# Attention with a mixture of experts on one core: VectorE copies the last transposed bank before the first block's maximum, and takes the norm sums and the token low parts in front of the context's copy

## The chip, the cores and the metric

The kernel runs on one core of a Trainium2 chip. The metric is the device time of one execution in microseconds; three runs of the kernel before gave 652.37, 653.87 and 654.20 us, with a median of 653.87 us. Everything below about where time goes comes from one further execution, taken by the hardware profiler: it took 654.04 us, and its span from the first to the last instruction is 652.0 us.

## The reference

Sixteen batches of 256 tokens with 128 channels go through a pre-norm block: causal attention with 16 heads (key width 8, value width 64), then a mixture of 8 experts that each pick their own 64 tokens.

```python
x = x + attn(layernorm(x), Wq, Wk, Wv, Wo)
x = x + ffn(layernorm(x), gate_w, w1, w2)

# attn: B, T, D = 16, 256, 128; H, DK, DV = 16, 8, 64
q, k, v = heads(x @ Wq), heads(x @ Wk), heads(x @ Wv)
attn = softmax(where(causal, -inf, q @ k.T / sqrt(DK)))
return (attn @ v) @ Wo

# ffn: E = 8, capacity 64 tokens of a batch for each expert
probs = softmax(x @ gate_w)
top_p, top_idx = top_k(probs.T, 64)
y = gelu(x[top_idx] @ w1) @ w2 * top_p
out[top_idx] += y
```

## The kernel before, in words

`attention` does the first half and the norm and the gate product of the second; `experts` follows it. The change is in `attention` alone, and there in VectorE's program alone.

**Units.** The 16 heads are cut in 4 groups of 4 heads, so that there are 64 units (`u = 4 * b + j`, with `b` the batch and `j` from 0 to 3). Each engine has its own program, written out by hand: a loop over `b` from -2 to 18 (the middle ones by a hardware loop), and in it the four values of `j`. The engines meet at semaphores only. In the step `u` an engine works on several units at once, each at another stage: queries and keys of `u + 2` (and on TensorE the product for `u + 3`), scores and exponentials of `u + 1`, transposed probabilities of `u - 1`, the context of `u - 2`.

**One unit.** TensorE makes the product for queries and keys (L635), ScalarE takes its high part (`qk_hi`, L352), VectorE the two low parts `qT` and `kT` (L449, L452). GpSimd spreads the keys over the heads' rows (`k_diag`, L303 and L305). TensorE multiplies: `s0_ps` are the scores of the first 128 queries (L620, L621), `s1_ps` those of the second 128 (L555 to L563). VectorE takes each row's maximum (L457 for the second block, L498 for the first), ScalarE the exponentials and their sums (L340), VectorE the reciprocals (`inv`, L480 and L522), GpSimd the normed probabilities (`probn`, L295 for the first block and L320 for the second). TensorE transposes them in three banks: two with L579 and L580, the third with L614. ScalarE copies two of the banks into `probT` (L362, L380), VectorE the third (L519). TensorE makes the context (L597), and VectorE copies it into `ctxT` (L486).

**Once for each batch.** At `j == 2` VectorE takes the sums of the first norm for batch `b + 2` (`norm_stats`, L505 to L511), GpSimd makes their root (L309, L311), and at `j == 0` of the next batch VectorE norms the tokens (`xn1`, L490, by the helper's line L434) and TensorE transposes them (L644). After the output product (L542) and the first residual (L476) at `j == 3`, VectorE takes the sums of the second norm (L512 to L515), GpSimd makes their root at `j == 0` (L314, L316), VectorE norms at `j == 1` (`xn2`, L495, again L434), and TensorE transposes (L650). ScalarE writes the high part of these tokens at `j == 2` (`xg_hi`, L383) and VectorE the low part (`xg_lo`, L503).

**What orders VectorE's work around the change.** Its instructions run in the written order. In a step this is: `qT` and `kT`; the second block's maximum (L457); one small piece by `j`; the first reciprocal (L480); the context's copy (L486); the norm itself at `j == 0` and `j == 1`; the first block's maximum (L498); then the low part and the sums; the third bank's copy (L519); the second reciprocal (L522). GpSimd's order in a step is `probn` of the first block (L295), `k_diag` (L303, L305), the roots, `probn` of the second block (L320).

Of the kernel before, what the change touches and what calls it, by code (L numbers as in the profile page):

```python
# [9 lines left out]
ALU = mybir.AluOpType  # L10
# [4 lines left out]
B, T, D = 16, 256, 128  # L15
TB = T // P
# [5 lines left out]
UNITS = B * G  # L22
# [8 lines left out]
def has(index, n):  # L31

    return not isinstance(index, int) or 0 <= index < n

def await_count(engine, sem, count):

    if not isinstance(count, int) or count > 0:
        engine.wait_ge(sem, count)
# [10 lines left out]
def f32(ap):  # L50
    return ap.bitcast(F32)
# [29 lines left out]
def attention(nc, x_tiles, w_q, w_k, w_v, w_o, gate_w, w1, w2,  # L81
# [5 lines left out]
    with ExitStack() as ctx:  # L87
# [34 lines left out]
        bn6 = sb("bn6", [P, TB, 6])  # L122
        mv1 = sb("mv1", [P, TB, 2])
# [3 lines left out]
        bn6b = sb("bn6b", [P, TB, 6])  # L127
        mv2 = sb("mv2", [P, TB, 2])
# [260 lines left out]
        def _(dve):  # L389
# [31 lines left out]
            def norm_stats(src, bn, mv, bn_done, bn_count, stats_done):  # L421
                nc.vector.memset(holds_wait[:, :], 0.0)
                for tb in range(TB):
                    last = nc.vector.bn_stats(bn[:, tb, :], src(tb))
                last.then_inc(bn_done, 1)
                dve.wait_ge(bn_done, bn_count)
                nc.vector.memset(holds_wait[:, :], 0.0)
                for tb in range(TB):
                    last = nc.vector.bn_aggr(mv[:, tb, :], bn[:, tb, :])
                last.then_inc(stats_done, 1)  # L430

            def norm(dst, src, mv, rstd, done):
                for tb in range(TB):
                    last = nc.vector.tensor_scalar(dst[:, tb, :], src(tb), mv[:, tb, 0:1], rstd[:, tb:tb + 1],  # L434
                                                   ALU.subtract, ALU.mult)
                last.then_inc(done, 1)

            def batch(b, par):
                for j in range(G):
                    u = b * G + j  # L440
                    r1, r2, rm = (j + 1) % RING, j % RING, (j + 1) % RING
                    if has(u + 2, UNITS):
                        w = u + 2
                        qk_ps = misc_ps[(3 * j) % 2][:, :].rearrange("p (a t) -> p a t", a=2)
                        dve.wait_ge(qk_hi_done, w + 1)
                        await_count(dve, s1_done, w - 1)
                        await_count(dve, k_ready, w - 1)

                        nc.vector.scalar_tensor_tensor(out=qT[r2][:, :], in0=f32(qk_hi[r2][:, 0, :]),  # L449
                                                       scalar=minus_low[:, 0:1], in1=qk_ps[:, 0, :],  # L450
                                                       op0=ALU.mult, op1=ALU.add)
                        nc.vector.scalar_tensor_tensor(out=kT[r2][:, :], in0=f32(qk_hi[r2][:, 1, :]),  # L452
                                                       scalar=minus_low[:, 1:2], in1=qk_ps[:, 1, :],
                                                       op0=ALU.mult, op1=ALU.add).then_inc(qk_ready, 1)
                    if has(u + 1, UNITS):
                        dve.wait_ge(s1_done, u + 2)
                        nc.vector.tensor_reduce(out=neg_max[:, r1, 1, :], in_=s1_ps[:, :, :], axis=AX.X,  # L457
                                                op=ALU.max, negate=True).then_inc(max1, 1)

                    extra = misc_ps[(3 * j + 1) % 2]  # L460
                    if j == 0 and has(b - 3, B):
                        dve.wait_ge(gate_done, b - 2)
                        nc.vector.tensor_copy(gate_logit[:, bass.ds((b - 3) * TB, TB), :],
                                              extra[:, 0:TB * E].rearrange("p (t e) -> p t e", t=TB)).then_inc(gate_ready, 1)
                    if j == 1 and has(b + 1, B):
                        dve.wait_ge(xT_hi_done, b + 2)
                        nc.vector.tensor_tensor(xT_lo[1 - par][:, :], extra[:, 0:T], f32(xT_hi[1 - par][:, :]),  # L467
                                                ALU.subtract).then_inc(xT_ready, 1)
                    if j == 2 and has(b - 2, B):
                        dve.wait_ge(x2T_done, b - 1)  # L470
                        await_count(dve, gate_done, b - 2)
                        nc.vector.tensor_copy(xn2T[:, :], extra[:, 0:T]).then_inc(x2T_ready, 1)  # L472
                    if j == 3 and has(b - 1, B):
                        tiles = bass.ds((b - 1) * TB, TB)
                        dve.wait_ge(wo_done, b)
                        nc.vector.tensor_tensor(x_all[:, tiles, :], extra[:, 0:T].rearrange("p (t d) -> p t d", t=TB),  # L476
                                                x_all[:, tiles, :], ALU.add).then_inc(x1_ready, 1)
                    if has(u + 1, UNITS):
                        dve.wait_ge(exp0, u + 2)
                        nc.vector.reciprocal(inv[:, r1, 0, :], sums[:, r1, 0, :]).then_inc(inv0, 1)  # L480
                    if has(u - 2, UNITS):
                        cb = par if j >= 2 else 1 - par
                        g = (j - 2) % G
                        dve.wait_ge(ctx_done, u - 1)
                        await_count(dve, wo_done, b - 1 if j >= 2 else b - 2)
                        nc.vector.tensor_copy(ctxT[cb][:, 2 * g:2 * g + 2, :], ctx_ps[:, :, :]).then_inc(ctx_ready, 1)  # L486
                    if j == 0 and has(b + 1, B):
                        dve.wait_ge(rstd1_done, b + 2)
                        await_count(dve, xT_done, b + 1)
                        norm(xn1, lambda tb: x_all[:, (b + 1) * TB + tb, :], mv1, rstd1, xn1_ready)  # L490
                    if j == 1 and has(b - 2, B):
                        dve.wait_ge(rstd2_done, b - 1)
                        await_count(dve, x2T_done, b - 2)
                        await_count(dve, xg_lo_done, b - 2)
                        norm(xn2, lambda tb: x_all[:, (b - 2) * TB + tb, :], mv2, rstd2, xn2_ready)  # L495
                    if has(u + 2, UNITS):
                        dve.wait_ge(s0_done, u + 3)
                        nc.vector.tensor_reduce(out=neg_max[:, r2, 0, :], in_=s0_ps[:, :, :], axis=AX.X,  # L498
                                                op=ALU.max, negate=True).then_inc(max0, 1)
                    if j == 2 and has(b - 2, B):  # L500
                        dve.wait_ge(xg_hi_done, b - 1)
                        tiles = bass.ds((b - 2) * TB, TB)
                        nc.vector.tensor_tensor(xg_lo[:, tiles, :], xn2[:, :, :], f32(xg_hi[:, tiles, :]),  # L503
                                                ALU.subtract).then_inc(xg_lo_done, 1)
                    if j == 2 and has(b + 2, B):  # L505
                        if isinstance(b, int) and b == -2:
                            dve.wait_ge(x_loaded[0], 16)
                        if isinstance(b, int) and b == 2:
                            for i in range(1, 4):
                                dve.wait_ge(x_loaded[i], 16)  # L510
                        norm_stats(lambda tb: x_all[:, (b + 2) * TB + tb, :], bn6, mv1, bn1_done, b + 3, stats1)  # L511
                    if j == 3 and has(b - 1, B):  # L512
                        dve.wait_ge(x1_ready, b)
                        await_count(dve, rstd2_done, b - 1)
                        norm_stats(lambda tb: x_all[:, (b - 1) * TB + tb, :], bn6b, mv2, bn2_done, b, stats2)  # L515
                    if has(u - 1, UNITS):
                        dve.wait_ge(t_done, (u - 1) * 3 + 3)
                        await_count(dve, ctx_done, u - 2)
                        nc.vector.tensor_copy(probT[rm][:, 1024:1536], t_ps[rm][:, :]).then_inc(t_dve, 1)  # L519
                    if has(u + 1, UNITS):  # L520
                        dve.wait_ge(exp1, u + 2)
                        nc.vector.reciprocal(inv[:, r1, 1, :], sums[:, r1, 1, :]).then_inc(inv1, 1)  # L522
# [517 lines left out]
```

## Time and profile before

| | |
|---|---|
| median of three runs | 653.87 us (652.37 to 654.20) |
| profiled execution | 654.04 us, span 652.0 us |
| TensorE matmul busy | 587.1 us, 90% of the span |
| VectorE busy | 433.9 us, 67% |
| ScalarE busy | 418.0 us, 64% |
| GpSimd busy | 350.2 us, 54% |
| mean granted clock of TensorE | 0.974 of full speed |

The attention half runs to about 475 us, in a pattern that repeats every 27.5 us (one batch, four steps). The experts take the rest. A row of the timeline gives the start and the length of an instruction, its engine, its line, what it writes and reads, and how long its engine had idled before it and for whom; instructions overlap at their edges by some 0.08 us. A busy TensorE does not mean a TensorE without pauses: a pause shorter than the modelled end of the matmul before it does not show as idle time, only as a wider distance between two starts.

### The profile page before, as it was taken

How to read it: one execution, taken by the hardware profiler on the slowest of the kernel's cores; microseconds unless marked ns; L12 is line 12 of the kernel's file. 1: busy time of each engine (PE TensorE's matmuls, PEld its weight loads, DVE VectorE, ACT ScalarE, POOL GpSimd, SP SyncE). 2: the span in 40 equal slices, each digit the busy share in tenths (PEclk: the TensorE clock that was granted, in tenths of full speed). 3: DMA queues.
4: the chain of work that ended last, by engine and by line, in shares of the span. 5: the costliest groups of instructions: out<-in, count | busy, mean ns of one | idle time of the engine just before them, and what ended most of it. 6: DMA issues, size and time to landing. Idle time of an engine off the chain costs nothing. (4 is left out here: it accounts for less than half of the span.)

```text
span 652.0 us, 15348 instructions
## 1 busy us (share of the span) xinstructions
PE 587.1 (90%) x5252; PEld 481.3 (74%) x5252; DVE 433.9 (67%) x1073; ACT 418.0 (64%) x1418; POOL 350.2 (54%) x373
## 2 busy tenths in 40 slices
PE   1799999999999999999999999999615999999996
PEld 1577877778777787877878778787503898989896
DVE  3578687787877878788787877966476233434245
ACT  2599797787977878778787787877021643334330
POOL 4577677666776768667686686766160010111111
PEclk9999999999999999999999999999956999999998
DMA  9600000000000000000000000000002100100001
GB/s 269 190 2 1 2 3 2 1 2 2 2 2 0 0 0 0 0 0 0 0 0 0 0 0 0 2 1 1 2 0 65 34 19 13 30 17 10 17 18 50
DMA packets 13548, 12.28 MB, mean 19 GB/s; under 512 B 832, under 2 KB 10304, under 8 KB 13504
## 3 DMA queue, kind: packets, MB, share of 16 engines
q1 hardware_dynamic: 13504, 11.69, 6.1%
q8 instruction: 28, 0.46, 0.3%
q14 instruction: 16, 0.13, 0.1%
HBM read 9.57 MB, written 2.11 MB: 18 GB/s over the span
## 5 line engine op out<-in xcount | busy, mean ns | idle before, releaser
L340 ACT ACTIVATE prob<-s_ps,neg_max 128x128 f32<-128x128 f32 (+1 forms) x512 | 209.0, 430 | 28.5 <-DVE neg_max L457 20.5
L303 POOL TENSOR_TENSOR k_diag<-kT,own_block 128x512 fp32r<-128x512 f32 x64 | 66.5, 1040 | 116.2 <-DVE kT L452 115.0
L320 POOL TENSOR_TENSOR probn<-prob,inv 128x1024 f32<-128x1024 f32 x64 | 121.2, 1894 | 2.6 <-DVE inv L522 2.6
L340 ACT ACTIVATION_READ_ACCUMULATOR prob<-s_ps,neg_max 128x1 f32 x512 | 110.2, 215 | 0.0
L597 PE MATMUL ctx_ps<-probT,v_sb 128*64 128x256 f32 (+1 forms) x1024 | 97.3, 332 | 0.8 <-DVE probT L519 0.8
L798 POOL TENSOR_TENSOR y_parts<-y_sb,y_parts 128x512 fp32r<-128x512 f32 x16 | 20.6, 1286 | 137.9 <-ACT y_parts L814 137.9
L597 PEld LDWEIGHTS ctx_ps<-probT,v_sb 128*64 128x64 f32 x1024 | 63.5, 136 | 30.0 <-issue 11.6
L457 DVE TENSOR_REDUCE neg_max<-s_ps 128x4 f32<-128x1024 f32 x64 | 77.8, 1216 | 0.4 <-PE s_ps L563 0.3
L498 DVE TENSOR_REDUCE neg_max<-s_ps 128x4 f32<-128x512 f32 x64 | 44.0, 688 | 48.4 <-PE s_ps L621 48.4
L295 POOL TENSOR_TENSOR probn<-prob,inv 128x512 f32<-128x512 f32 x64 | 66.6, 1040 | 11.5 <-PE t_ps L614 11.5
L486 DVE COPY ctxT<-ctx_ps 128x512 f32<-128x512 f32 x64 | 44.2, 690 | 33.2 <-PE ctx_ps L597 32.0
L362 ACT ACTIVATE probT<-t_ps 128x512 f32<-128x512 f32 x64 | 39.0, 609 | 41.1 <-PE t_ps L580 41.1
L579 PE MATMUL t_ps<-ident,probn 128*128 128x128 f32 x256 | 63.8, 287 | 1.3 <-DVE probT L519 1.0
L542 PE MATMUL misc_ps<-wo_sb,ctxT 128*128 128x128 f32 x512 | 63.5, 278 | 0.6 <-DVE xn2T L472 0.6
L542 PEld LDWEIGHTS misc_ps<-wo_sb,ctxT 128*128 128x128 f32 x512 | 59.6, 191 | 2.2 <-issue 0.8
L580 PE MATMUL t_ps<-ident,probn 128*128 128x128 f32 x256 | 60.2, 273 | 0.0
L1005 PE MATMUL y_ps<-w_sb,w_raw 128*64 128x128 f32 x1024 | 59.4, 274 | 0.0
L1005 PEld LDWEIGHTS y_ps<-w_sb,w_raw 128*64 128x64 f32 x1024 | 55.6, 137 | 2.2
L822 ACT ACTIVATE xin_hi<-pick_hi_ps 128x512 fp32r<-128x512 f32 x16 | 9.6, 599 | 72.4 <-PE pick_lo_ps L969 72.4
L833 ACT ACTIVATE w_raw<-h_ps 128x512 f32<-128x512 f32 x64 | 38.2, 598 | 26.1 <-PE h_ps L990 23.7
L535 PE MATMUL misc_ps<-xT_hi,wqk_hi 128*128 128x256 f32 x128 | 49.7, 388 | 1.0 <-DVE xT_lo L467 1.0
L352 ACT ACTIVATE qk_hi<-misc_ps 128x512 fp32r<-128x512 f32 x64 | 39.1, 611 | 15.6 <-PE misc_ps L537 15.4
(153 smaller groups left out, 1386.4 us busy)
## 6 DMA issues: line engine op xcount, KB each, us to landing
x_all<-in_L_attn_x SPq DMA_DIRECT2D x4, 512.0 KB, 6.9
w_raw<-in_L_ffn_w SPq DMA_DIRECT2D x1, 2048.0 KB, 12.0
toks<-tok_rows SPq DMA_DIRECT2D x8, 256.0 KB, 3.2
out<-x_all SPq DMA_DIRECT2D x16, 128.0 KB, 1.8
wv_raw<-in_L_attn_Wv SPq DMA_DIRECT2D x1, 512.0 KB, 5.0
wo_sb<-in_L_attn_Wo SPq DMA_DIRECT2D x1, 512.0 KB, 5.6
wqk_raw<-in_L_attn_Wq SPq DMA_DIRECT2D x1, 64.0 KB, 3.3
wqk_raw<-in_L_attn_Wk SPq DMA_DIRECT2D x1, 64.0 KB, 3.4
```

Source lines behind the costliest of these rows:

```text
L295: nc.gpsimd.tensor_tensor(probn[r][:, 0:HG * P].rearrange("p (i k) -> p i k", i=HG), prob[r][:, 0:HG * P].rearrange("p (i k) -> p i k", i=HG),
L303: nc.gpsimd.tensor_tensor(k_diag0[r][:, :, :], bcast(f32(kT[r][:, 0:P]), 1, HG), bcast(own_block[:, :], 2, P), ALU.mult)
L320: nc.gpsimd.tensor_tensor(probn[r][:, HG * P:].rearrange("p (i k) -> p i k", i=HG), prob[r][:, HG * P:].rearrange("p (i k) -> p i k", i=HG ...
L340: last = nc.scalar.activation(prob[r][:, first + i * keys:first + (i + 1) * keys], scores[:, i, :], ACT.Exp, bias=neg_max[:, r, block_, i: ...
L457: nc.vector.tensor_reduce(out=neg_max[:, r1, 1, :], in_=s1_ps[:, :, :], axis=AX.X, op=ALU.max, negate=True).then_inc(max1, 1)
L486: nc.vector.tensor_copy(ctxT[cb][:, 2 * g:2 * g + 2, :], ctx_ps[:, :, :]).then_inc(ctx_ready, 1)
L535: nc.tensor.matmul(out_, w_h, x_h, start=True, stop=False)
L542: last = nc.tensor.matmul(to[:, tb * D:(tb + 1) * D], context[:, c, tb * P:(tb + 1) * P], wo_sb[:, c, :], start=(c == 0), stop=(c == chunk ...
L579: nc.tensor.transpose(t[:, i, 0:P], q0[:, 2 * f + i, :], ident[:, :])
L580: last = nc.tensor.transpose(t[:, i, P:T], q1[:, 2 * f + i, 0:P], ident[:, :])
L597: last = nc.tensor.matmul(ctx_ps[half * DV:(half + 1) * DV, pair, kb * P:T], v_sb[vb][:, kb, h * DV:(h + 1) * DV], rhs, start=(kb == 0), s ...
L1005: last = nc.tensor.matmul(y_ps[half * CAP:(half + 1) * CAP, q, :], hT[m % RING][:, half, c, q * CAP:(q + 1) * CAP], w2_sb[:, 2 * (m % EP) ...
```

## The change

Three things move in VectorE's program, and nothing is added or taken away. The copy of the third transposed bank (L519 before, L515 after) now comes ahead of the first block's maximum (L498 before, L518 after) in every step. The norm sums at `j == 2` and `j == 3` come right after the first reciprocal, ahead of the context's copy (L486 before, L502 after). The low part `xg_lo` goes from `j == 2` to `j == 3` (L503 before, L484 after), also ahead of the context's copy.

```diff
                     if has(u + 1, UNITS):
                         dve.wait_ge(exp0, u + 2)
                         nc.vector.reciprocal(inv[:, r1, 0, :], sums[:, r1, 0, :]).then_inc(inv0, 1)
+                    if j == 3 and has(b - 2, B):
+                        dve.wait_ge(xg_hi_done, b - 1)
+                        tiles = bass.ds((b - 2) * TB, TB)
+                        nc.vector.tensor_tensor(xg_lo[:, tiles, :], xn2[:, :, :], f32(xg_hi[:, tiles, :]),
+                                                ALU.subtract).then_inc(xg_lo_done, 1)
+                    if j == 2 and has(b + 2, B):
...
+                        norm_stats(lambda tb: x_all[:, (b + 2) * TB + tb, :], bn6, mv1, bn1_done, b + 3, stats1)
+                    if j == 3 and has(b - 1, B):
+                        dve.wait_ge(x1_ready, b)
+                        await_count(dve, rstd2_done, b - 1)
+                        norm_stats(lambda tb: x_all[:, (b - 1) * TB + tb, :], bn6b, mv2, bn2_done, b, stats2)
                     if has(u - 2, UNITS):
...
                         norm(xn2, lambda tb: x_all[:, (b - 2) * TB + tb, :], mv2, rstd2, xn2_ready)
+                    if has(u - 1, UNITS):
+                        dve.wait_ge(t_done, (u - 1) * 3 + 3)
+                        await_count(dve, ctx_done, u - 2)
+                        nc.vector.tensor_copy(probT[rm][:, 1024:1536], t_ps[rm][:, :]).then_inc(t_dve, 1)
                     if has(u + 2, UNITS):
                         dve.wait_ge(s0_done, u + 3)
                         nc.vector.tensor_reduce(out=neg_max[:, r2, 0, :], in_=s0_ps[:, :, :], axis=AX.X,
                                                 op=ALU.max, negate=True).then_inc(max0, 1)
-                    if j == 2 and has(b - 2, B):
-                        dve.wait_ge(xg_hi_done, b - 1)
...
-                    if j == 2 and has(b + 2, B):
...
-                    if j == 3 and has(b - 1, B):
...
-                    if has(u - 1, UNITS):
-                        dve.wait_ge(t_done, (u - 1) * 3 + 3)
-                        await_count(dve, ctx_done, u - 2)
-                        nc.vector.tensor_copy(probT[rm][:, 1024:1536], t_ps[rm][:, :]).then_inc(t_dve, 1)
```

First place: VectorE from `j == 3` into `j == 0` of a batch in the steady part, before the change, from the first reciprocal on.

```order
L480 RECIPROCAL inv<-sums 128x4
L486 COPY ctxT<-ctx_ps 128x512
L498 TENSOR_REDUCE neg_max<-s_ps 128x4
L422 MEMSET holds_wait 128x1
L424 BN_STATS bn6b<-x_all 128x6 x2
L427 MEMSET holds_wait 128x1
L429 BN_AGGR mv<-bn6b 128x2 x2
L519 COPY probT<-t_ps 128x512
L522 RECIPROCAL inv<-sums 128x4
L449 SCALAR_TENSOR_TENSOR qT<-qk_hi,minus_low,misc_ps 128x256
```

The same place after the change.

```order
L480 RECIPROCAL inv<-sums 128x4
L484 TENSOR_TENSOR xg_lo<-xn,xg_hi 128x256
L422 MEMSET holds_wait 128x1
L424 BN_STATS bn6b<-x_all 128x6 x2
L427 MEMSET holds_wait 128x1
L429 BN_AGGR mv<-bn6b 128x2 x2
L502 COPY ctxT<-ctx_ps 128x512
L515 COPY probT<-t_ps 128x512
L518 TENSOR_REDUCE neg_max<-s_ps 128x4
L522 RECIPROCAL inv<-sums 128x4
L449 SCALAR_TENSOR_TENSOR qT<-qk_hi,minus_low,misc_ps 128x256
```

The sums and the low part are now ahead of the context's copy, and between the first block's maximum and the next step's `qT` only the reciprocal is left.

Second place: VectorE in `j == 0`, before the change, from the context's copy to the next step's `kT`.

```order
L486 COPY ctxT<-ctx_ps 128x512
L434 TENSOR_SCALAR xn<-x_all,mv,rstd 128x128 x2
L498 TENSOR_REDUCE neg_max<-s_ps 128x4
L519 COPY probT<-t_ps 128x512
L522 RECIPROCAL inv<-sums 128x4
L449 SCALAR_TENSOR_TENSOR qT<-qk_hi,minus_low,misc_ps 128x256
L452 SCALAR_TENSOR_TENSOR kT<-qk_hi,minus_low,misc_ps 128x256
```

The same place after the change.

```order
L502 COPY ctxT<-ctx_ps 128x512
L434 TENSOR_SCALAR xn<-x_all,mv,rstd 128x128 x2
L515 COPY probT<-t_ps 128x512
L518 TENSOR_REDUCE neg_max<-s_ps 128x4
L522 RECIPROCAL inv<-sums 128x4
L449 SCALAR_TENSOR_TENSOR qT<-qk_hi,minus_low,misc_ps 128x256
L452 SCALAR_TENSOR_TENSOR kT<-qk_hi,minus_low,misc_ps 128x256
```

The norm (two instructions of L434) keeps its place behind the context's copy; the bank's copy and the maximum behind it have changed places. The orders of the other four engines are the same in both kernels.

## Rows read from the trace of the kernel before

**Rows 1.** Busy time by stretch: stretch, length, busy us (x instructions) of each engine, clock, DMA.
```profile
269.10:275.20 6.10, 6.10 (x53) 4.72 (x52) 5.40 (x18) 5.01 (x20) 3.71 (x6) 1.00 0.00 0
275.20:281.70 6.50, 6.01 (x52) 4.51 (x50) 6.25 (x12) 6.32 (x23) 6.23 (x6) 1.00 0.00 0
```

**Rows 2.** Waits of TensorE, 44 to 434 us: line, releaser, total, times, longest.
```profile
PE misc_ps L650 <- issue: 3.6, 7, 0.6
PE misc_ps L650 <- DVE xn L434: 2.9, 6, 0.6
...
PEld t_ps L579 <- DVE probT L519: 0.9, 2, 0.4
```

**Rows 3.** Timeline of TensorE, two steps of batch 9.
```profile
270.54 0.27 PE L580 MATMUL t_ps<-ident,probn 128*128 128x128 f32 x1
270.72 0.33 PE L579 MATMUL t_ps<-ident,probn 128*128 128x128 f32 x1
...
275.22 0.43 PE L644 MATMUL misc_ps<-ident,xn 128*128 128x128 f32 x2
...
281.70 0.41 PE L650 MATMUL misc_ps<-ident,xn 128*128 128x128 f32 x2 [0.49 <-issue]
```

**Rows 4.** Timeline of VectorE over the same steps.
```profile
266.86 0.69 DVE L486 COPY ctxT<-ctx_ps 128x512 f32<-128x512 f32 x1 [1.71 <-PE ctx_ps L597]
268.65 0.69 DVE L498 TENSOR_REDUCE neg_max<-s_ps 128x4 f32<-128x512 f32 x1 [1.10 <-PE s_ps L621]
...
269.97 0.69 DVE L519 COPY probT<-t_ps 128x512 f32<-128x512 f32 x1
...
270.66 0.45 DVE L449 SCALAR_TENSOR_TENSOR qT<-qk_hi,minus_low,misc_ps 128x256 fp32r<-128x256 f32 x1
...
272.87 0.69 DVE L486 COPY ctxT<-ctx_ps 128x512 f32<-128x512 f32 x1
273.48 0.59 DVE L434 TENSOR_SCALAR xn<-x_all,mv,rstd 128x128 f32 x2
...
276.10 0.48 DVE L449 SCALAR_TENSOR_TENSOR qT<-qk_hi,minus_low,misc_ps 128x256 fp32r<-128x256 f32 x1
...
281.52 0.68 DVE L498 TENSOR_REDUCE neg_max<-s_ps 128x4 f32<-128x512 f32 x1
```

**Rows 5.** Single instructions of the norm: first of `j == 0`, both of `j == 1`.
```profile
273.48 0.34 DVE L434 TENSOR_SCALAR xn<-x_all,mv,rstd 128x128 f32 x1
...
279.35 1.25 DVE L434 TENSOR_SCALAR xn<-x_all,mv,rstd 128x128 f32 x1
...
280.52 1.08 DVE L434 TENSOR_SCALAR xn<-x_all,mv,rstd 128x128 f32 x1
```

**Rows 6.** Timeline of ScalarE: the high part of queries and keys.
```profile
269.44 0.60 ACT L352 ACTIVATE qk_hi<-misc_ps 128x512 fp32r<-128x512 f32 x1 [0.60 <-PE misc_ps L537]
...
275.44 0.63 ACT L352 ACTIVATE qk_hi<-misc_ps 128x512 fp32r<-128x512 f32 x1
```

**Rows 7.** Timeline of GpSimd over the same steps.
```profile
271.58 1.04 POOL L303 TENSOR_TENSOR k_diag<-kT,own_block 128x512 fp32r<-128x512 f32 x1 [2.31 <-DVE kT L452]
...
274.07 1.90 POOL L320 TENSOR_TENSOR probn<-prob,inv 128x1024 f32<-128x1024 f32 x1
...
277.05 1.04 POOL L303 TENSOR_TENSOR k_diag<-kT,own_block 128x512 fp32r<-128x512 f32 x1
...
278.62 1.89 POOL L320 TENSOR_TENSOR probn<-prob,inv 128x1024 f32<-128x1024 f32 x1
280.47 1.04 POOL L295 TENSOR_TENSOR probn<-prob,inv 128x512 f32<-128x512 f32 x1
...
283.71 1.04 POOL L303 TENSOR_TENSOR k_diag<-kT,own_block 128x512 fp32r<-128x512 f32 x1 [2.20 <-DVE kT L452]
```

**Rows 8.** Timeline of the last batches: one on TensorE, one on VectorE.
```profile
458.67 0.33 PE L579 MATMUL t_ps<-ident,probn 128*128 128x128 f32 x1 [0.64 <-DVE probT L519]
...
465.85 0.41 DVE L503 TENSOR_TENSOR xg_lo<-xn,xg_hi 128x256 fp32r<-128x256 f32 x1
```

More of the change, by code:

```diff
@@ L480, in batch @@
                         nc.vector.reciprocal(inv[:, r1, 0, :], sums[:, r1, 0, :]).then_inc(inv0, 1)
+                    if j == 3 and has(b - 2, B):
[4 more added lines that the diff above has]
+                    if j == 2 and has(b + 2, B):
+                        if isinstance(b, int) and b == -2:
+                            dve.wait_ge(x_loaded[0], 16)
+                        if isinstance(b, int) and b == 2:
+                            for i in range(1, 4):
+                                dve.wait_ge(x_loaded[i], 16)
+                        norm_stats(lambda tb: x_all[:, (b + 2) * TB + tb, :], bn6, mv1, bn1_done, b + 3, stats1)
[3 more added lines that the diff above has]
+                        norm_stats(lambda tb: x_all[:, (b - 1) * TB + tb, :], bn6b, mv2, bn2_done, b, stats2)
                     if has(u - 2, UNITS):
@@ L499, in batch @@
                                                 op=ALU.max, negate=True).then_inc(max0, 1)
-                    if j == 2 and has(b - 2, B):
-                        dve.wait_ge(xg_hi_done, b - 1)
-                        tiles = bass.ds((b - 2) * TB, TB)
-                        nc.vector.tensor_tensor(xg_lo[:, tiles, :], xn2[:, :, :], f32(xg_hi[:, tiles, :]),
-                                                ALU.subtract).then_inc(xg_lo_done, 1)
-                    if j == 2 and has(b + 2, B):
[L506 to L511, printed above, removed]
-                    if j == 3 and has(b - 1, B):
-                        dve.wait_ge(x1_ready, b)
-                        await_count(dve, rstd2_done, b - 1)
-                        norm_stats(lambda tb: x_all[:, (b - 1) * TB + tb, :], bn6b, mv2, bn2_done, b, stats2)
-                    if has(u - 1, UNITS):
-                        dve.wait_ge(t_done, (u - 1) * 3 + 3)
-                        await_count(dve, ctx_done, u - 2)
-                        nc.vector.tensor_copy(probT[rm][:, 1024:1536], t_ps[rm][:, :]).then_inc(t_dve, 1)
                     if has(u + 1, UNITS):
```

## The prediction

> **What bounds the kernel now.** I read the busy time by stretch first. In the two steps shown TensorE is busy 6.10 of 6.10 us and 6.01 of 6.50 us, at full clock; VectorE idles in the first and is nearly full in the second [rows 1]. So the attention half runs at TensorE's pace, and a change on VectorE is worth only what it takes from, or adds to, TensorE's pauses. I read TensorE's waits next. Over 390 us of attention it idles 3.6 + 2.9 us ahead of the transposes of the second norm's tokens (L650), in 13 pauses, once for each batch, and for VectorE's third bank 0.9 us in the two longest pauses [rows 2]. The timeline adds a pause too short to count as idle: in `j == 0` the second group of transposes starts 0.18 us after the instruction before it, where others follow at 0.11, and the next distance is 0.16 instead of 0.11. It waits for VectorE's bank copy, which ends at 269.97 + 0.69 = 270.66 [rows 3, 4]. That is 0.12 us for each batch.
>
> The larger pause, at L650, is the most instructive thing in this trace. The norm of `j == 1` ends at 280.52 + 1.08 = 281.60, and L650 starts at 281.70 [rows 3, 5]. The same two instructions take 0.59 us in `j == 0` and 2.25 us in `j == 1`: the first 1.25 instead of 0.34, the second 1.08 [rows 4, 5]. The lengths fit GpSimd's: L320 ends at 278.62 + 1.89 = 280.51 and the first norm instruction 0.09 later, L295 ends at 280.47 + 1.04 = 281.51 and the second also 0.09 later [rows 5, 7]. So a norm instruction that starts under a GpSimd product stands still until that product ends, and a product that is pending gets in between the two. In `j == 0` they escape, since they end at 274.07, just where L320 begins [rows 4, 7]. Copies out of PSUM and maxima show no such stretch.
>
> The Trainium skill (SBUF — State Buffer, "Who interferes with whom") says that a VectorE instruction in a two-port mode and a GpSimd instruction exclude each other, and that whoever issues first holds the pair for the whole instruction. The lengths above agree with it.
>
> **The change part by part.** It adds no instruction. The terms are what moves in time.
>
> *Copy before maximum.* Both stay on VectorE (0.69 us each, next start 0.6 us later), and the bank is ready before the scores are. So the copy fills a part of the 1.10 us for which the maximum waited [rows 4], and the maximum is late by the rest of the copy at most: 0.15 us in most steps, 0.6 in `j == 1`, where both were queued already. There ScalarE's first exponentials come 0.6 us later. I cost this at nothing: their readers on TensorE come more than 1 us later. If that cover failed, it would be up to 0.6 us a batch.
>
> *Sums and low part ahead of the context's copy.* In `j == 3` they cost 0.73 and 0.35 us and fall into the 1.71 us for which VectorE waited for the context [rows 4]. Ahead of L486 they need 1.1 of it. The low part reads two tensors that both lie in SBUF, and L320 will be running by then; no row shows one fully inside such a product. From below it costs nothing more, from above it waits out the product, some 1.3 us; then `ctxT` comes 0.5 us late and the bank's copy still starts when its transposes are done. Nothing on TensorE waits for either, so the value is 0. In `j == 2` the sums (0.73 us) fit before the first maximum's scores in the same way.
>
> The Trainium skill (same page and section) says that two SBUF inputs also meet GpSimd's reads. By that rule the low part takes the upper end, and the sum stays as it is.
>
> *What comes free.* At the turn from `j == 3` to `j == 0` VectorE no longer has the sums and the copy behind the maximum. The maximum ends near 269.4, and `qT` then waits for ScalarE's high part alone, which ends at 269.44 + 0.60 = 270.04 [rows 6]. Where `qT` waits for it already it starts 0.03 us after it (275.44 + 0.63 = 276.07, then 276.10) [rows 4, 6]. So `qT` moves from 270.66 to 270.07. TensorE does not wait for it. GpSimd does: it idled 2.31 us for `kT` [rows 7]. From a waiting `qT` to L303 it is 277.05 - 276.10 = 0.95 us, and from L303 to L320 274.07 - 271.58 = 2.49 us [rows 4, 7]. L320 moves to 270.07 + 0.95 + 2.49 = 273.51, 0.56 us earlier.
>
> *What that collides with.* The norm in `j == 0` follows the context's copy, which is bound to TensorE: 273.48, less the 0.12 us that TensorE gains, is 273.36; its second instruction follows 0.59 - 0.34 = 0.25 us later, at 273.61 [rows 4, 5]. So L320 at 273.51 falls between the two. The first instruction gets through. The second stands until L320 ends, at 273.51 + 1.89 = 275.40, or up to 0.19 later if the first one holds the product back; it ends 0.09 later, at 275.49 to 275.68, and L644 can start 0.10 behind that, at 275.59 to 275.78. It started at 275.22 [rows 3]. After `j == 0` TensorE is 0.37 to 0.56 us late.
>
> Behind the norm stand the copy, the maximum, the reciprocal, `qT` and `kT` in VectorE's queue, and GpSimd behind `kT`. In `j == 1` of the kernel before it is 283.71 - 281.52 = 2.19 us from the release of that queue to L303 [rows 4, 7]. Now it is released at 275.40 to 275.59, and L303 comes at 277.59 to 277.78 instead of 277.05. L320 and L295 follow it back to back and end the norm of `j == 1`, so L650 is late by the same 0.54 to 0.73 us. It contains the delay of `j == 0`. I take 0.64 us a batch.
>
> Over the batches: the roots that set L320's time at `j == 0` are there from batch 2. In batch 2 the pause that goes is 0.4 us and the norm escapes; that leaves batches 3 to 14, twelve of them: 12 x 0.64 = 7.7 us.
>
> *Gains once.* Two long pauses for the third bank go: 0.9 us [rows 2]. In the tail another goes, 0.64 us and 0.06 of restart [rows 8]; the low part that now comes ahead of the last batch's sums is on the chain there and costs 0.35 to 0.41 [rows 8]. Together 1.2 us; GpSimd's earlier product in batch 15 gives perhaps 0.3. That is 1.5 us.
>
> Sum against the profiled execution: 654.0 + 7.7 - 1.5 = 660.2 us. It is 0.2 us above the median of the three runs, which changes nothing.
>
> **The rivals.** *A, the norm escapes (faster).* If L320 comes 0.1 us later than worked out, or VectorE keeps its turn over both instructions, nothing collides. Then the 0.12 us for each of 13 batches and the 1.5 us once are won: 654.0 - 1.6 - 1.5 = 650.9. For it: the margin is 0.10 us, and between batches the two starts differ by up to 0.06 us. Against it: L295 got in between two norm instructions when it had started just 0.05 us before the second (280.47 and 280.52) [rows 5, 7].
>
> The Trainium skill (as above) lets the one that issues first hold the pair. If that held for both norm instructions together, this case is what it would give, 650.9; rows 5 and 7 speak against it, since the product got in there.
>
> *C, both norm instructions lose (slower still).* If L320 comes more than 0.15 us earlier, both stand, the second behind L295 too, as in `j == 1`. The norm ends at 273.36 + 0.15 + 1.85 + 1.04 + 0.09, some 276.5, L644 at 276.6, and L303 in `j == 1` is 1.5 us late: 12 x 1.5 - 1.5 = 16.5, and 670.5.
>
> *D, mixed or hidden.* The starts vary, and some batches collide where others escape; with four to six colliding, or with a delay of half the size because VectorE makes it up in `j == 1`, it is 654 - 1.5 + 1 to 4: 652.5 to 655.8.
>
> **How the numbers follow.** The collision as worked out 0.50, A 0.28, D 0.14, C 0.08. A measurement of this kernel can tell some 0.3% from no change, which is 651.9 to 655.8. Faster is A and a little of D: 0.29. The same is nearly all of D and an edge of A: 0.15. Slower is the collision and C: 0.56. The likeliest case's own range is 657 to 664 (0.37 to 0.9 us a batch). The range for 8 in 10 takes in A and leaves C out: 650 to 666.
>
> **What would show it.** In the profile after, L434 in `j == 0` should read some 2.1 us for its two instructions instead of 0.59, the first at 0.3 to 0.4 and the second at 1.8, ending just behind an L320. `qT` should start 0.03 us behind ScalarE's high part. TensorE should wait for L434 ahead of L644 by about half a microsecond a batch, and longer than now ahead of L650. The distances of 0.18 us in the transposes of `j == 0` should be gone. If L434 stays at 0.59 us in `j == 0`, A holds and my step on the order of L320 and the norm was wrong. If a period takes the 27.5 us of before although L434 is stretched, the queue behind it was covered. If `qT` doesn't start at once, VectorE is held by something that I costed at nothing.

## The result: slower by 1.2%, and the profile after

The changed kernel takes 662.63 us (median of six runs, 661.17 to 664.13) against 654.53 us for the kernel before (six runs, 652.37 to 656.26): a ratio of 1.0124, 95% interval 1.0095 to 1.0153. The forecast was 660.2 us. The profiled execution took 664.13 us, with a span of 662.2 us.

The page's head and its busy times of the kernel after:

```profile
span 662.2 us, 15348 instructions
## 1 busy us (share of the span) xinstructions
PE 588.0 (89%) x5252; PEld 483.3 (73%) x5252; DVE 465.1 (70%) x1073; ACT 417.3 (63%) x1418; POOL 349.9 (53%) x373
```

With the same number of instructions VectorE is busy for 31.2 us more than before (433.9 us): 19.8 us of it in the norm (L434), 14.6 us in the low part (L484), and 3 us less elsewhere. The busy times of TensorE's matmuls, ScalarE and GpSimd stay within 1 us. So two things on VectorE got longer, and the waits of TensorE say which of them it waited for (44 to 444 us; they answer to [rows 2]):

```profile
PE misc_ps L644 <- DVE xn L434: 8.1, 13, 1.3
PE misc_ps L650 <- issue: 4.9, 7, 0.7
PE misc_ps L650 <- DVE xn L434: 4.0, 6, 0.7
```

The kernel before has one wait at L644 in its stretch (44 to 434 us):

```profile
PE misc_ps L644 <- DVE xn L434: 0.7, 1, 0.7
```

TensorE now idles 8.1 us in 13 waits for the norm of `j == 0` (L644) instead of 0.7 us in one, and 8.9 us instead of 6.5 ahead of L650. It waits for the low part nowhere. The timelines of one steady batch, engine by engine, with single norm instructions last (answer to [rows 3 to 7]; ScalarE first, then VectorE, GpSimd, TensorE):

```profile
273.58 0.60 ACT L352 ACTIVATE qk_hi<-misc_ps 128x512 fp32r<-128x512 f32 x1 [0.60 <-PE misc_ps L537]
```

```profile
274.37 0.48 DVE L449 SCALAR_TENSOR_TENSOR qT<-qk_hi,minus_low,misc_ps 128x256 fp32r<-128x256 f32 x1 [0.66 <-ACT qk_hi L352]
...
277.50 2.29 DVE L434 TENSOR_SCALAR xn<-x_all,mv,rstd 128x128 f32 x2
```

```profile
275.32 1.04 POOL L303 TENSOR_TENSOR k_diag<-kT,own_block 128x512 fp32r<-128x512 f32 x1 [1.90 <-DVE kT L452]
...
277.81 1.89 POOL L320 TENSOR_TENSOR probn<-prob,inv 128x1024 f32<-128x1024 f32 x1
```

```profile
274.68 0.27 PE L580 MATMUL t_ps<-ident,probn 128*128 128x128 f32 x1
274.79 0.27 PE L579 MATMUL t_ps<-ident,probn 128*128 128x128 f32 x1
...
279.84 0.44 PE L644 MATMUL misc_ps<-ident,xn 128*128 128x128 f32 x2 [0.48 <-DVE xn L434]
...
286.55 0.41 PE L650 MATMUL misc_ps<-ident,xn 128*128 128x128 f32 x2 [0.71 <-issue]
```

```profile
277.50 0.34 DVE L434 TENSOR_SCALAR xn<-x_all,mv,rstd 128x128 f32 x1
...
277.75 2.03 DVE L434 TENSOR_SCALAR xn<-x_all,mv,rstd 128x128 f32 x1
```

The norm of `j == 0` takes 2.29 us for its two instructions instead of 0.59. The first gets through in 0.34. The second stands until L320 ends (277.81 + 1.89 = 279.70) and ends 0.08 later. L644 follows at 279.84. The pause of 0.18 us between the two groups of transposes (L580, then L579) has become the ordinary 0.11.

Where the 10.2 us between the two spans came from can be read from the starts of L650. The first one of the steady part comes 0.8 us earlier (88.43 instead of 89.25), since the two long pauses for the third bank are gone. From there to the L650 of batch 15 it is 367.1 us instead of 357.4, 9.7 more: ten periods of 28.19 instead of 27.51 us (6.9), two of 28.96, each 1.5 more than before (3.0), less 0.2 in batch 15. From there to the last L650 it is 1.2 more, and in the experts 0.2. In the tail 0.7 us is won by the bank's copy, and the output products of the last batch take 1.6 us longer. The kernel before, then the kernel after:

```profile
466.08 3.81 PE L542 MATMUL misc_ps<-wo_sb,ctxT 128*128 128x128 f32 x32 [0.61 <-DVE xn2T L472]
```

```profile
474.28 5.44 PE L542 MATMUL misc_ps<-wo_sb,ctxT 128*128 128x128 f32 x32 [0.61 <-DVE xn2T L472]
```

The granted clock tells why. Two stretches of the kernel after (as [rows 1], the clock is the third figure from the end):

```profile
474.00:478.00 4.00, 3.72 (x19) 3.75 (x20) 0.13 (x1) 0.00 (x0) 0.00 (x0) 0.57 0.02 4
478.00:480.00 2.00, 2.00 (x20) 1.97 (x18) 0.24 (x1) 0.00 (x0) 0.00 (x0) 1.00 0.00 0
```

In the kernel before, the same products ran at 1.00; here half of them ran at the lower of the two levels, 0.21 us from start to start instead of 0.11. Of the six runs three have a span of 662.0 to 662.2 at a mean clock of 0.972 and three of 659.2 to 659.4 at 0.974 to 0.977, so it looks as if this comes and goes from run to run and isn't the order's doing; only one of the six was traced. Without the 1.6 us the profile's difference is 8.6 us, close to the medians' 8.1.

### The profile page after: what moved, and what is told of

The parts are those of the page before. It is cut to its first block and busy times, and to the rows that moved or that the text cites. A ratio compares the mean times of both kernels' runs of the same rounds, so it can differ in the third digit from the quotient of the medians.

```text
span 662.2 us, 15348 instructions
## 1 busy us (share of the span) xinstructions
PE 588.0 (89%) x5252; PEld 483.3 (73%) x5252; DVE 465.1 (70%) x1073; ACT 417.3 (63%) x1418; POOL 349.9 (53%) x373
## 5 line engine op out<-in xcount | busy, mean ns | idle before, releaser
L340 ACT ACTIVATE prob<-s_ps,neg_max 128x128 f32<-128x128 f32 (+1 forms) x512 | 209.2, 432 | 38.3 <-DVE neg_max L518 31.9
L303 POOL TENSOR_TENSOR k_diag<-kT,own_block 128x512 fp32r<-128x512 f32 x64 | 66.5, 1040 | 108.2 <-DVE kT L452 108.0
L320 POOL TENSOR_TENSOR probn<-prob,inv 128x1024 f32<-128x1024 f32 x64 | 121.2, 1894 | 1.5 <-DVE inv L522 1.4
L340 ACT ACTIVATION_READ_ACCUMULATOR prob<-s_ps,neg_max 128x1 f32 x512 | 111.7, 218 | 0.0
L434 DVE TENSOR_SCALAR xn<-x_all,mv,rstd 128x128 f32 (+1 forms) x64 | 65.7, 1067 | 2.2 <-POOL rstd L311 1.2
L542 PE MATMUL misc_ps<-wo_sb,ctxT 128*128 128x128 f32 x512 | 65.1, 282 | 0.6 <-DVE xn2T L472 0.6
L542 PEld LDWEIGHTS misc_ps<-wo_sb,ctxT 128*128 128x128 f32 x512 | 61.2, 196 | 2.2 <-issue 0.8
L579 PE MATMUL t_ps<-ident,probn 128*128 128x128 f32 x256 | 62.2, 283 | 0.1
L580 PE MATMUL t_ps<-ident,probn 128*128 128x128 f32 x256 | 59.4, 273 | 0.0
L502 DVE COPY ctxT<-ctx_ps 128x512 f32<-128x512 f32 x64 | 43.0, 671 | 13.4 <-PE ctx_ps L597 13.4
```

The costliest lines, as they stand in the source:

```text
L303: nc.gpsimd.tensor_tensor(k_diag0[r][:, :, :], bcast(f32(kT[r][:, 0:P]), 1, HG), bcast(own_block[:, :], 2, P), ALU.mult)
L320: nc.gpsimd.tensor_tensor(probn[r][:, HG * P:].rearrange("p (i k) -> p i k", i=HG), prob[r][:, HG * P:].rearrange("p (i k) -> p i k", i=HG ...
L340: last = nc.scalar.activation(prob[r][:, first + i * keys:first + (i + 1) * keys], scores[:, i, :], ACT.Exp, bias=neg_max[:, r, block_, i: ...
L542: last = nc.tensor.matmul(to[:, tb * D:(tb + 1) * D], context[:, c, tb * P:(tb + 1) * P], wo_sb[:, c, :], start=(c == 0), stop=(c == chunk ...
L579: nc.tensor.transpose(t[:, i, 0:P], q0[:, 2 * f + i, :], ident[:, :])
L580: last = nc.tensor.transpose(t[:, i, P:T], q1[:, 2 * f + i, 0:P], ident[:, :])
```

## The experiments

Three theories stood: the *collision* (`qT` comes early, GpSimd's product with it, and the norm of `j == 0` is caught), the *late maximum* (the copy ahead of the first block's maximum delays ScalarE; its waits for that maximum had indeed grown from 7.8 to 31.9 us, while those for the second block's had shrunk from 20.5 to 4.5), and the *moved sums* (work ahead of the context's copy). Ratios are against the kernel before on the same chip. The period is the mean distance of eleven starts of the second norm's transposes, and the offset is how long after the first norm instruction of `j == 0` GpSimd's long product (L320) starts.

### The copy alone, and the sums alone

```diff
 # e1_copy_only, against the kernel before
+                    (third bank's copy, L519)
                     (first block's maximum, L498)
                     (low part, sums)
-                    (third bank's copy, L519)
```

> Only the third bank's copy goes ahead of the first block's maximum; the norm sums and the low part stay where they were. Collision (the norm of j == 0 starts under GpSimd's second product because qT comes early): behind the maximum VectorE still has the sums of 0.73 us, so qT comes at about 270.25 in the old time frame instead of 270.66, and GpSimd's product at about 273.7, which is 0.1 us behind the second norm instruction. That is on the edge: in the changed kernel a lead of 0.07 us of the second norm instruction lost and one of 0.17 us won. I expect it to lose in most batches, 658 to 662 us, with a fair chance that it escapes, 652 to 655. Late maximum (the loss comes from the maximum that now waits behind the copy): the whole loss, 661 to 663. Moved sums (the loss comes from the sums and the low part ahead of the context's copy): 653 to 655.

Measured: 657.95 us, ratio 1.0040 (1.0025 to 1.0055), a third of the loss and just below the range for "most batches". The periods alternate between 27.4 and 28.2 us from batch 4 on, and so does the norm (timeline of VectorE, of two batches in a row):

```profile
219.07 2.30 DVE L434 TENSOR_SCALAR xn<-x_all,mv,rstd 128x128 f32 x2
...
247.29 0.59 DVE L434 TENSOR_SCALAR xn<-x_all,mv,rstd 128x128 f32 x2
```

GpSimd, at the same places:

```profile
219.39 1.90 POOL L320 TENSOR_TENSOR probn<-prob,inv 128x1024 f32<-128x1024 f32 x1
...
247.99 1.90 POOL L320 TENSOR_TENSOR probn<-prob,inv 128x1024 f32<-128x1024 f32 x1
```

With an offset of 0.32 us the second instruction is caught, with 0.70 both escape; a batch that was delayed leaves the next one with more room. The maximum is later in every batch (at `j == 2` and `j == 3` it starts 0.18 us behind its scores instead of 0.04, at `j == 1` 1.64 or 1.85 instead of 1.02), and the loss comes in every other one; no theory without the collision has that. "On the edge" was right; that it would alternate I had not seen.

```diff
 # e2_sums_only, against the changed kernel
-                    (third bank's copy, L515)
                     (first block's maximum, L518)
+                    (third bank's copy, L515)
```

> Only the norm sums and the low part go ahead of the context's copy; the bank's copy stays behind the first block's maximum. Collision: between the maximum and qT are now the copy and the reciprocal, and they end ahead of ScalarE's high part, so qT starts as early as in the changed kernel, and the collision is complete: 660 to 663 us, with the norm of j == 0 at 2.3 us. Late maximum: no loss, 653 to 655. Moved sums: the whole loss, 661 to 663, but then without a stretched norm.

Measured: 662.84 us, ratio 1.0118 (1.0085 to 1.0150); the periods are 28.2 us, with 29.0 for the two of batches 3 and 14 and 27.25 for batch 4 (28.11 on the mean). The maximum is ahead of the copy again and the whole loss is there, so the late maximum is out. The norm is stretched to 2.29 us from batch 5 to 13, and to 3.06 in 3 and 14; in 4 it escapes. Batch 9:

```profile
276.04 2.29 DVE L434 TENSOR_SCALAR xn<-x_all,mv,rstd 128x128 f32 x2
```

### Two ways out of the collision

```diff
 # e3_gpsimd_later, against the changed kernel (GpSimd, j == 0; the new tile and semaphore are left out here)
                         nc.gpsimd.tensor_tensor(rstd2[:, :], var2[:, :], neg_half[:, :], ALU.pow).then_inc(rstd2_done, 1)
+                        nc.gpsimd.tensor_tensor(idle_sb[:, :], eps_sb[:, :], neg_half[:, :], ALU.add).then_inc(idle_done, 1)
+                        pool.wait_ge(idle_done, b - 1)
```

> The changed kernel with one more tiny instruction on GpSimd (a sum of 128x2 elements into an unused tile, and a wait for it) between the root of the second norm and the product of the second block at j == 0, once a batch. It puts the product some 0.27 us later, from 0.31 to about 0.58 us behind the first norm instruction, and 0.33 behind the second. Collision: work added to GpSimd frees the norm, L434 reads 0.59 us at j == 0, the period falls from 28.2 to 27.4 us, and the time to 651 to 654. Late maximum and moved sums: nothing changes, 662 to 664.

Measured: 652.50 us, ratio 0.9962 (0.9943 to 0.9981). One useless instruction on GpSimd makes the changed kernel 10 us faster. GpSimd's and VectorE's timelines:

```profile
271.41 0.19 POOL L319 TENSOR_TENSOR idle_sb<-eps_sb,neg_half 128x2 f32<-128x2 f32 x1
271.68 1.90 POOL L324 TENSOR_TENSOR probn<-prob,inv 128x1024 f32<-128x1024 f32 x1
```

```profile
271.10 0.59 DVE L438 TENSOR_SCALAR xn<-x_all,mv,rstd 128x128 f32 x2
```

The offset is 0.58 and the norm back at 0.59 us; the period is 27.2 to 27.3. Only batches 3 and 14, where the offset is 0.35, still collide (two periods of 28.23).

```diff
 # e4_norm_first, against the changed kernel
+                    (norm of j == 0, L487 to L490 of the kernel before)
                     (context's copy, L502)
-                    (norm of j == 0)
```

> The changed kernel with the norm of j == 0 ahead of the context's copy instead of behind it. It now starts near the end of GpSimd's second k_diag instruction, stands until that ends (0.5 us at most), and is done before the long product starts; the context's copy comes 0.4 us late, which nothing waits for. Collision: 651 to 654 us, the period 27.4. Late maximum and moved sums: 662 to 664.

Measured: 649.26 us, ratio 0.9918 (0.9891 to 0.9945), below the range. The norm stands 0.2 us at the end of the short key product and is through long before the long one:

```profile
269.45 0.61 POOL L305 TENSOR_TENSOR k_diag<-kT,own_half 128x256 fp32r<-128x256 f32 x1
...
270.95 1.90 POOL L320 TENSOR_TENSOR probn<-prob,inv 128x1024 f32<-128x1024 f32 x1
```

```profile
269.59 0.81 DVE L434 TENSOR_SCALAR xn<-x_all,mv,rstd 128x128 f32 x2
```

It escapes in every batch from 2 to 14, in 3 and 14 too; in batches 0 and 1 it is caught (2.49 us). Batches 3 and 14 are 1.9 of the 3.2 us between it and the kernel with GpSimd later; the rest isn't explained here. Both theories without the collision wanted 662 to 664 in both kernels.

The control puts the same small instruction (the diff of e3) into the kernel before.

> A control for the kernel with GpSimd later: the same tiny instruction and wait at the same place in the kernel before. There the norm of j == 0 escapes already, so there is nothing to free. Collision: the long product and the one behind it come 0.27 us later, the keys' product of j == 1 behind them too (it had 0.08 us to spare), and with them the norm of j == 1 and L650: 0.1 to 0.2 us a batch, 655 to 658 us. Rival (a later GpSimd is good in itself): faster by 3 us or more, as the changed kernel was with it.

Measured: 655.12 us, ratio 1.0015 (1.0003 to 1.0027), and the period goes from 27.51 to 27.64. A later GpSimd is worth nothing in itself; it costs 0.13 us a batch, since its queue in `j == 1` then has no idle time left ahead of the keys' product (0.08 us in the kernel before).

### A form of the norm that isn't caught

```diff
 # v1_before_accum, v2_after_accum (both norms; the new tile is left out here)
                     last = nc.vector.tensor_scalar(dst[:, tb, :], src(tb), mv[:, tb, 0:1], rstd[:, tb:tb + 1],
-                                                   ALU.subtract, ALU.mult)
+                                                   ALU.subtract, ALU.mult, accum_out=unused[:, tb:tb + 1])
```

> The kernel before, with an accumulator output (into an unused tile of two columns) on the two norm instructions and nothing else changed. Lock (a norm instruction can't run beside a GpSimd product, because of the form it takes): if this form runs beside the product, L434 at j == 1 reads 0.6 to 0.9 us instead of 2.25, the pause of 0.6 us ahead of L650 goes in 13 batches, and the time falls by 7 to 8 us to 646 to 648. Rival (the norm is slow beside GpSimd whatever its form): L434 at j == 1 stays at 2.2 us and the time at 654 to 656. The Trainium skill (SBUF — State Buffer, Who interferes with whom) excepts the form that writes out its accumulator from the two-port modes, which speaks for the first.

Measured: 643.23 us, ratio 0.9834 (0.9803 to 0.9865), period 26.81.

> The changed kernel with the same accumulator output on the norm and nothing else changed. Lock: both stretched norms go, that of j == 0 too, so the change shows only what it was without the collision. The period falls from 28.2 us to that of the kernel with GpSimd later (27.25) less the pause ahead of L650 (0.6), so 26.6 to 26.8 us, and the time to 642 to 646. Rival (form makes no difference): 661 to 664.

Measured: 638.32 us, ratio 0.9763 (0.9729 to 0.9796), period 26.55. Both are some 3 to 4 us below their ranges: I had counted the steady batches alone, and the norms of batches 0, 1 and 15 were caught as well (2.49, 2.37 and 2.37 us in the kernel before). In v1 the first L650 comes 1.4 us earlier than in the kernel before, and batch 15 is 1.1 us shorter. VectorE's timeline, with the norms of `j == 0` and `j == 1`:

```profile
264.50 0.40 DVE L435 TENSOR_SCALAR_CACHE_REDUCE xn<-x_all,mv,rstd 128x128 f32 x1
264.83 0.40 DVE L435 TENSOR_SCALAR_CACHE_REDUCE xn<-x_all,mv,rstd 128x128 f32 x1
...
270.26 0.40 DVE L435 TENSOR_SCALAR_CACHE_REDUCE xn<-x_all,mv,rstd 128x128 f32 x1
270.58 0.40 DVE L435 TENSOR_SCALAR_CACHE_REDUCE xn<-x_all,mv,rstd 128x128 f32 x1
```

GpSimd's products beside them:

```profile
264.82 1.90 POOL L321 TENSOR_TENSOR probn<-prob,inv 128x1024 f32<-128x1024 f32 x1
...
269.54 1.90 POOL L321 TENSOR_TENSOR probn<-prob,inv 128x1024 f32<-128x1024 f32 x1
```

Each instruction takes 0.40 us, 0.06 more than the plain form, also under a product that is running (269.54 to 271.44). So a norm instruction stands only when both come together, the plain form and a GpSimd product beside it. The Trainium skill (SBUF — State Buffer, "Who interferes with whom") excepts this form from the two-port modes, and these rows agree. The pair also prices the change without its collision: 638.32 against 643.23, 4.9 us faster.

```diff
 # v3_norm_first_accum: v2, the norm of j == 0 as in e4, and at j == 3
-                    (low part)
                     (sums of the second norm)
+                    (low part)
```

> The changed kernel with the norm of j == 0 ahead of the context's copy, the accumulator output on the norm, and the low part behind the sums at j == 3 instead of ahead of them. If the lock is all that the order of the norm was about, the order adds nothing once the form is free: the same as the changed kernel with the accumulator output, within 1 us, and 0.3 us less in the tail from the low part. If the norm's place has a worth of its own (the kernel with the norm first was 3 us faster than that with GpSimd later), it is 2 to 3 us faster than that one: 640 to 643 us.

Measured: 638.30 us, ratio 0.9759 (0.9735 to 0.9783), period 26.55: the same as v2. So the norm's place is worth nothing except that it avoids the collision.

### A version that beats both

```diff
 # v4_two_pass (on v3's order, plain norm at j == 0), v5_before_two_pass (on the kernel before); for j == 1 (the call, the tile and the semaphore are left out here):
+            def norm_two(dst, src, mv, rstd, half, count, done):
+                for tb in range(TB):
+                    last = nc.vector.tensor_scalar(dst[:, tb, :], src(tb), mv[:, tb, 0:1], rstd[:, tb:tb + 1],
+                                                   ALU.subtract, ALU.mult, accum_out=unused[:, tb:tb + 1])
+                last.then_inc(half, 1)
+                dve.wait_ge(half, count)
+                for tb in range(TB):
+                    last = nc.vector.tensor_scalar(dst[:, tb, :], dst[:, tb, :], rstd[:, tb:tb + 1], rstd[:, tb:tb + 1],
+                                                   ALU.mult, ALU.mult, accum_out=unused[:, TB + tb:TB + tb + 1])
+                last.then_inc(done, 1)
```

> A version that should beat both kernels. The changed kernel with the norm of j == 0 ahead of the context's copy, the low part behind the sums at j == 3, and the norm of j == 1 in two passes of the form with an accumulator output, that don't stand still beside a GpSimd product: the first subtracts the mean, the second multiplies by the root. In the kernel with the norm first the norm of j == 1 takes 2.26 us and L650 waits for it; four instructions of 0.33 us and a wait between the passes are 1.4 us, 0.85 less, and the pause of 0.55 us goes. Lock: the period falls from 27.26 us to 26.6 to 26.8, and the time from 649.3 to 642 to 644 us (13 batches of 0.55, and up to 1.6 us given back in the tail, where the two last norms of this kind are on the chain). Rival (the gain of the accumulator form lay in the product that it leaves out): 648 to 650.

Measured: 641.52 us, ratio 0.9787 (0.9757 to 0.9816), with the whole computation in it, and half a microsecond below the range. Four instructions are faster here than two. VectorE's norm of `j == 1` and TensorE's transposes behind it:

```profile
270.81 0.40 DVE L442 TENSOR_SCALAR_CACHE_REDUCE xn<-x_all,mv,rstd 128x128 f32 x1
...
271.91 0.40 DVE L447 TENSOR_SCALAR_CACHE_REDUCE xn<-xn,rstd 128x128 f32<-128x128 f32 x1
```

```profile
272.49 0.38 PE L663 MATMUL misc_ps<-ident,xn 128*128 128x128 f32 x2
```

The norm ends at 272.31, and the transposes at 272.49 follow without idle time; the period is 26.54, as in v2.

> The kernel before with the same two passes for the norm of j == 1 and nothing else changed. Its norm of j == 0 escapes as before, so only the pause ahead of L650 (0.6 us, 13 batches) goes, and the tail gives up to 1.6 us back: 646 to 649 us, period 26.8 to 26.95. The difference between this kernel and the other one of this call (the change, the norm's place and the low part's) should be 4 to 5 us, as between the two with the accumulator output.

Measured: 645.68 us, ratio 0.9848 (0.9821 to 0.9875), period 26.81, just below the range. It is slower than v4 by 4.2 us, near the 4.9 between v1 and v2.

## Why the prediction was right, point by point

**The pause ahead of L650 and its cause.** Right. The lengths of the norm follow the ends of GpSimd's products in every kernel with the plain form, and the pause goes with the form alone (v1, v4, v5).

**`qT` moves, and GpSimd's product with it.** Right in kind; the size was 0.16 us off in ten of the twelve batches. I let `qT` start 0.03 us behind ScalarE's high part. It starts at 274.37, 0.19 behind 273.58 + 0.60. From `qT` to L303 (0.95) and from there to L320 (2.49) is as predicted. So the offset is 0.31 us in most batches, not 0.15. The 0.19 goes with the hardware loop, which runs batches 4 to 13: there it is 0.19 to 0.21 us in every `j == 0`, and in batches 2, 3, 14 and 15, whose code is written out, 0.03. Batch 3, ScalarE and then VectorE:

```profile
103.58 0.60 ACT L352 ACTIVATE qk_hi<-misc_ps 128x512 fp32r<-128x512 f32 x1 [0.52 <-PE misc_ps L537]
```

```profile
104.20 0.48 DVE L449 SCALAR_TENSOR_TENSOR qT<-qk_hi,minus_low,misc_ps 128x256 fp32r<-128x256 f32 x1 [0.43 <-ACT qk_hi L352]
```

It isn't how long VectorE had idled: in batch 0 of the kernel before that was 1.14 us, and `qT` started 0.03 behind too. In the loop two instructions of VectorE's sequencer (L39, the wait for a count) stand between the end of the high part and `qT`, and in batch 3 none; that they are the cause is likely, but no run tests it. The offset is 0.08 us in batches 3 and 14 and 0.31 to 0.33 from 4 to 13; 0.16 of the difference is this delay. In v2, where nothing collides, these offsets are the same within 0.01 us, so it isn't a collision that sets them.

**Which instruction loses.** The outcome was right in ten batches, but my step ("L320 falls between the two") rested on recorded starts, and these don't decide alone. The second norm instruction started at 277.75, 0.06 us ahead of L320, and lost. A step that was sized wrong and a rule that was too simple cancelled here, and that is luck: with the offset that was measured, my rule would have let the norm escape in most batches, and in batches 3 and 14, where `qT` did start 0.03 behind, both instructions lost. What decides, over batches 2 to 14 of the kernels with the plain form and the norm behind the context's copy, is the lead that each instruction has over the product by its recorded start: with 0.05 to 0.08 us it is caught, with 0.09 (once, e2 in batch 4) and with 0.15 and more it escapes. So both are caught at an offset of 0.08 us (in batch 3 the first read 2.05 us although it had started ahead of the product), the second at 0.21 to 0.33, and neither from 0.41 on. At 0.34 (e2, escaped) and 0.35 (e3, caught twice) the lead of the second was 0.09 and 0.08.

**The price of a batch.** 0.64 us predicted, 0.68 measured, in ten batches. In two (3 and 14) both instructions were caught and the price was 1.5 us, which is rival C's. I had all twelve at the likeliest price: 1.7 us of the miss. The spans differ by 10.2 us where the forecast was 6.2; the rest of these 4.0 us is 0.4 in the ten batches, 1.6 for the clock in the tail, 0.2 in the experts and 0.1 of the gains. As a whole C did not come, nor A in more than batch 2, where it was predicted.

**Copy before maximum.** Costed at nothing, and e2 bears it out: without it the caught batches have the same period (28.20 and 28.19 us). ScalarE waits 24 us more for this maximum, 16 us less for the other, and TensorE doesn't wait for ScalarE.

**The low part ahead of the context's copy.** No row of before showed it inside a product. It takes the upper end: at 269.21 it stood 1.61 us, under an L320 that had started at 268.65.

```profile
269.21 1.61 DVE L484 TENSOR_TENSOR xg_lo<-xn,xg_hi 128x256 f32 x1
```

It takes 1.6 to 1.7 us in twelve batches instead of 0.43. It cost the end nothing, as predicted (v3 has it behind the sums, in `j == 3`, and the same period as v2). The Trainium skill's rule on two SBUF inputs, which I had set beside the bounds, agrees.

**Gains once.** Predicted 1.5 us. The first L650 shows 0.8, the tail's pause 0.7, batch 15 0.2, less 0.3 for the low part: 1.4 us.

**D and the sign.** The mixed case is what the copy alone gives (e1). The sign was right: +6.2 us forecast, +8.1 between the medians.

## What to carry to other kernels

Before moving work on VectorE forward, ask who starts earlier by it. Put GpSimd's long SBUF instructions and those of VectorE that can be caught on one timeline and read the distance between them: half a microsecond can be the whole protection (here an offset of 0.59 us). In these traces the ones that can be caught are the plain norm (TENSOR_SCALAR) and the low part (TENSOR_TENSOR of two SBUF inputs), and not the norm sums (L424), which read one SBUF input too. VectorE and GpSimd at `j == 3` of batch 1 in the kernel after:

```profile
72.26 0.29 DVE L424 BATCH_NORM_STATS2 bn6b<-x_all 128x6 f32<-128x128 f32 x1
```

```profile
71.54 1.89 POOL L320 TENSOR_TENSOR probn<-prob,inv 128x1024 f32<-128x1024 f32 x1
```

The sums take 0.27 to 0.29 us wherever they stand. Where a norm like this must run beside GpSimd and its result is waited for, a slower form that isn't caught (0.40 instead of 0.34 us) can be much faster than the fast one. An idle time that disappears is no gain until the end of what it released has been followed to the engine that sets the pace.
